# One order of the matmul queue for another in the memory loop: weights turned ahead of their products, activations turned between products, one gradient moved up, one product of zeros left out

## The reference

```python
def _mlp(params, h):
    for w1, w2 in params:
        h = h + jax.nn.gelu(h @ w1) @ w2
    return h
def assoc_loss(p, k, v):
    return jnp.mean((_mlp(p, k) - v) ** 2)
def step(carry, x_t):                       # 16 steps, one for each image row
    params, mom = carry                     # ((w1_0, w2_0), (w1_1, w2_1)), one set for each of 8 images
    k = _l2norm(x_t @ Wk); v = x_t @ Wv     # lr, forget, eta: means of sigmoids of x_t
    g = grad_fn(params, k, v)
    new_mom    = eta * mom - lr * g
    new_params = params * (1 - forget) + new_mom
(paramsT, _), _ = jax.lax.scan(step, (params0, mom0), x)
out = _mlp(mean of paramsT over the images, q)
```

## Time and profile before

| | |
|---|---|
| runs (3) | 324.80, 324.86, 325.09 us; median 324.86 |
| profiled execution | 322.84 us |
| its span, first to last instruction | 321.0 us (1.84 us lie around it) |
| memory loop in the span | 51.9 to 212.9 us, 16 steps |
| mean granted clock of PE | 0.979 of full speed |
| PE busy in the span | 280.7 us, 87% |

### The profile page before, as it was taken

The page is one execution under the profiler, slowest core; times in us unless marked ns, Lnnn a source line. Parts: engine busy times, 40 slices in busy tenths (PEclk is TensorE's granted clock), DMA queues, the critical chain, the costliest instruction groups (busy, mean ns, idle before and its releaser), DMA issues.

```text
span 321.0 us, 8491 instructions
## 1 busy us (share of the span) xinstructions
PE 280.7 (87%) x3338; PEld 186.9 (58%) x3345; DVE 212.1 (66%) x392; ACT 144.6 (45%) x353; POOL 145.6 (45%) x227
## 2 busy tenths in 40 slices
PE   8698759999999999999999999979985774899992
PEld 3233545777777777777777777754333552446642
DVE  0827554656666566665666656675478699899995
ACT  2003554466454664546655466523311662078511
POOL 8300087776667766677666776650000067200000
PEclk9999977999999999999999999999999998999998
DMA  7000000000000000000000000000000000000001
GB/s 289 14 0 2 0 1 2 0 0 0 0 0 0 0 0 0 0 0 0 0 0 0 0 0 0 0 2 2 0 0 2 0 2 0 1 2 0 0 0 65
DMA packets 874, 3.09 MB, mean 10 GB/s; under 512 B 96, under 2 KB 96, under 8 KB 864
## 3 DMA queue, kind: packets, MB, share of 16 engines
q1 hardware_dynamic: 864, 2.96, 2.5%
HBM read 2.44 MB, written 0.52 MB: 9 GB/s over the span
## 4 chain that ended last, share of the span: by engine, by line
PE 68%; DVE 23%; ACT 3%; issue 3%; POOL 2%; DVEq 0%; POOLq 0%
PE ps L1100 16%; PE ps L1082 9%; PE ps L1091 9%; PE ps L1110 6%; DVE arena_mem L754 4%; PE ps L1287 3%; PE ps L968 3%; PE ps L1318 2%; DVE arena_att L830 2%; PE ps L1166 2%; PE ps L993 2%; PE ps L1211 2%; DVE uf L850 1%; PE ps L1326 1%; ACT act_u L471 1%
## 5 line engine op out<-in xcount | busy, mean ns | idle before, releaser
L968 PE MATMUL ps<-zero 128*128 128x512 bf16 x130 | 34.7, 412 | 5.2 <-DVE uf L850 2.9
L350 POOL TENSOR_TENSOR arena_mem<-arena_mem,keep_e 128x512 f32<-128x512 f32 x32 | 33.4, 1043 | 0.0
L359 POOL TENSOR_TENSOR arena_mem<-arena_mem,keep_d 128x512 f32<-128x512 f32 x32 | 33.3, 1040 | 0.0
L747 DVE TENSOR_TENSOR arena_mem<-ps,arena_mem 128x512 f32<-128x512 f32 x49 | 32.0, 681 | 0.0
L481 ACT ACTIVATE arena_mem<-ps 128x512 f32<-128x512 f32 x48 | 28.7, 597 | 7.1 <-PE ps L1100 5.0
L1100 PE MATMUL ps<-const_sb,arena_mem 128*128 128x128 f32 x192 | 31.5, 287 | 0.0
L968 PEld LDWEIGHTS ps<-zero 128*128 128x128 bf16 x137 | 13.6, 106 | 24.6 <-issue 9.2
L471 ACT ACTIVATE act_u<-ps 128x128 f32<-128x128 f32 x32 | 8.9, 277 | 38.1 <-PE ps L1082 38.1
L366 POOL TENSOR_SCALAR z_e<-z_sq 128x128 f32<-128x128 f32 x32 | 9.5, 298 | 33.4 <-ACT z_sq L472 33.3
L1091 PE MATMUL ps<-act_u,arena_mem 128*64 128x16 f32 x512 | 20.6, 211 | 2.3
L1091 PEld LDWEIGHTS ps<-act_u,arena_mem 128*64 128x64 f32 x512 | 18.0, 137 | 7.7 <-issue 6.6
(11 more groups left out here) (267 smaller groups left out, 634.0 us busy)
## 6 DMA issues: line engine op xcount, KB each, us to landing
param_sb<-param SPq DMA_DIRECT2D x1, 840.5 KB, 7.2
arena_conv<-band SPq DMA_DIRECT2D x1, 576.0 KB, 5.6
xs_sb<-xs SPq DMA_DIRECT2D x1, 512.0 KB, 3.2
out<-xh SPq DMA_DIRECT2D x2, 256.0 KB, 2.1
const_sb<-const SPq DMA_DIRECT2D x1, 449.5 KB, 4.1
```

What stands on the lines that cost most here:

```text
L350: pool.tensor_tensor(qe[:, m, :].rearrange("p (b d) -> p b d", b=8), we[:, m, :].rearrange("p (b d) -> p b d", b=8), keep_e[:, bass.ts(t, ...
L359: pool.tensor_tensor(by_pair(kept), by_pair(w), keep_d[:, bass.ts(t, J)].unsqueeze(2).broadcast_to([P, J, E1]), ALU.mult).then_inc(sem("ke ...
L747: dve.tensor_tensor(by_pair(w11 if m == 1 else we[:, m, :]), momentum(m), by_pair(qe[:, m, :]), ALU.add)\
L968: pe.matmul(ps[:, bank, :], zero_bf[:, 0:P], zero_bf[:, :], start=True, stop=True)
```

## The change

On PE, in a step:

- w20 is turned right after z0, in the place of the product of zeros; w21 right after h1; w11 after h2. Each thus stands one product ahead of where a weight was turned, in another order of weights (w20, w21, w11 instead of w11, w21, w20), and the banks of PSUM are swapped.
- The activations are turned in pairs or singly: `u0`, `h1bd` after x; `u1`, `k_now` behind the turn of w11; `rbd` after `plus`. So `tok_lr` now holds u1 in the place of rbd, and `tok_raw` gets rbd by an ACT copy of its own (`r_tok`) and two others together.
- `plus` waits for `y1` instead of `slope1`, since the tanh of the second layer now goes to SBUF (`z_t1`) instead of PSUM.
- g21 stands ahead of the turn of `dhbd`; the other three gradients stay behind du0.

On DVE `updated(2)` goes ahead of the first `arg`, `updated(1)` moves from the end of a step into the next one, and the `mom_scale`s stand in another order. On POOL w21 is decayed before w11. ACT's copies follow PE's new order. The first w11 is now made by an update from its kept copy, like the first w21.

PE from z0 to x, first before and then of the change; `arena_mem` holds the weights, and the waits of each piece stand with its first row.

The diff, cut to its core:

```diff
@@ POOL, before the loop
-            pool.tensor_copy(by_pair(w11), ...).then_inc(sem("w11_new"), 1)
+            pool.tensor_copy(by_pair(qe[:, 1, :]), ...).then_inc(sem("kept_w11_new"), 1)
@@ POOL
                 kept_hidden(0, "w20_new")
+                kept_hidden(2, "w21_new")
                 kept_channels(qe[:, 1, :], w11, "w11_new", t + 1)
-                kept_hidden(2, "w21_new")
@@ ACT
                 hidden(0, "z0_done", "u0_ready", "z0_sq")
+                turned(7, 0, "w20_tp", "w20_d", -0.5)
                 evicted(h1bd[:, :], 5, 0, "h1_ps", "h1_ready")
-                turned(6, 1, "w11_tp", "w11_e")
+                turned(6, 2, "w21_tp", "w21_d", -0.5)
                 hidden(1, "z1_done", "u1_ready", "z1_sq")
-                turned(7, 2, "w21_tp", "w21_d", -0.5)
+                tanh(0, z_t0[:, 0, :], "y0", "tanh0")
                 evicted(rbd[:, :], 5, 0, "h2_ps", "r_ready")
                 tanh(1, th1, "y1", "tanh1")
-                tanh(0, z_t0[:, 0, :], "y0", "tanh0")
-                turned(6, 0, "w20_tp", "w20_d", -0.5)
+                turned(7, 1, "w11_tp", "w11_e")
                 act.wait_ge(sem("lr_tp"), t + 1)
-                act.activation(tok_lr[:, :, :], ps[:, 7, :]...
+                act.activation(tok_lr[:, :, :], ps[:, 6, :]...
+                evicted(tok_raw[:, 0, :], 7, 0, "r_tp", "r_tok")
                 evicted(dhbd[:, :], 4, 3 * P, "dh1_ps", "dh1_ready")
                 act.wait_ge(sem("raw_tp"), t + 1)
-                act.activation(tok_raw[:, 0:3, :], ps[:, 6, 0:3 * P]...
+                act.activation(tok_raw[:, 1:3, :], ps[:, 7, P:3 * P]...
-                evicted(dh_tok[:, :], 7, 0, "dh1_tp", "dh_tok")
+                evicted(dh_tok[:, :], 6, 0, "dh1_tp", "dh_tok")
@@ DVE
+                updated(2, "w21_new", "g21", t + 1)
                 arg(0, "z0_sq", "y0")
-                updated(2, "w21_new", "g21", t + 1)
+                updated(1, "w11_new", "g11", t + 1)
                 mom_scale(1)
+                mom_scale(2)
                 arg(1, "z1_sq", "y1")
-                mom_scale(2)
+                mom_scale(0)
...
                 mom_scale(3)
-                mom_scale(0)
...
                 updated_w10(t + 1)
                 updated(0, "w20_new", "g20", t + 1)
-                updated(1, "w11_new", "g11", t + 1)
             updated(2, "w21_new", "g21", NS + 1)
+            updated(1, "w11_new", "g11", NS + 1)
@@ PE
                 pe.wait_ge(sem("kbd_ready"), 4)
-                fill(7, 0, BANK)
                 pe.wait_ge(sem("w20_new"), t + 1)
+                turn_weights(7, we[:, 0, :]).then_inc(sem("w20_tp"), 1)
                 pe.wait_ge(sem("u0_ready"), t + 1)
                 by_image(5, 0, we[:, 0, :], act_u[:, 0, :]).then_inc(sem("h1_ps"), 1)
+                pe.wait_ge(sem("w21_new"), t + 1)
+                turn_weights(6, we[:, 2, :]).then_inc(sem("w21_tp"), 1)
+                pe.wait_ge(sem("x_now"), t + 1)
+                pe.wait_ge(sem("y0"), t + 1)
                 pe.wait_ge(sem("w11_new"), t + 1)
-                turn_weights(6, w11).then_inc(sem("w11_tp"), 1)
-                pe.wait_ge(sem("y0"), t + 1)
                 pe.wait_ge(sem("h1_ready"), t + 1)
                 by_halves(4, P, w11, h1bd).then_inc(sem("z1_done"), 1)
-                pe.wait_ge(sem("x_now"), t + 1)
-                pe.wait_ge(sem("w21_new"), t + 1)
-                turn_weights(7, we[:, 2, :]).then_inc(sem("w21_tp"), 1)
...
+                pe.wait_ge(sem("w21_d"), t + 1)
+                for n, x in enumerate((act_u[:, 0, :], h1bd)):
+                    turn(6, n * P, x[:, :])
                 pe.wait_ge(sem("u1_ready"), t + 1)
                 by_image(5, 0, we[:, 2, :], act_u[:, 1, :]).then_inc(sem("h2_ps"), 1)
-                pe.wait_ge(sem("w11_e"), t + 1)
-                turn_weights(6, we[:, 0, :]).then_inc(sem("w20_tp"), 1)
-                pe.wait_ge(sem("w21_d"), t + 1)
+                pe.wait_ge(sem("w20_d"), t + 1)
+                turn_weights(7, w11).then_inc(sem("w11_tp"), 1)
+                turn(6, 2 * P, act_u[:, 1, :])
+                turn(6, 3 * P, k_now[:, :]).then_inc(sem("lr_tp"), 1)
                 pe.wait_ge(sem("r_ready"), t + 1)
                 by_halves(5, 2 * P, wd[:, 2, :], rbd).then_inc(sem("du1_done"), 1)
-                for n, x in enumerate((act_u[:, 0, :], h1bd, rbd, k_now)):
-                    mm = turn(7, n * P, x[:, :])
-                mm.then_inc(sem("lr_tp"), 1)
-                pe.wait_ge(sem("slope1"), t + 1)
+                pe.wait_ge(sem("y1"), t + 1)
                 plus(4, 3 * P, rbd[:, :], True)
+                pe.wait_ge(sem("w11_e"), t + 1)
+                turn(7, 0, rbd[:, :]).then_inc(sem("r_tp"), 1)
                 pe.wait_ge(sem("dz1_ready"), t + 1)
                 by_image(4, 3 * P, we[:, 1, :], dz1).then_inc(sem("dh1_ps"), 1)
-                pe.wait_ge(sem("w20_d"), t + 1)
-                turn(6, 0, act_u[:, 1, :])
-                turn(6, P, dz1[:, :])
+                pe.wait_ge(sem("r_tok"), t + 1)
+                turn(7, P, dz1[:, :])
                 pe.wait_ge(sem("slope0"), t + 1)
-                turn(6, 2 * P, z_p[:, 0, :]).then_inc(sem("raw_tp"), 1)
+                turn(7, 2 * P, z_p[:, 0, :]).then_inc(sem("raw_tp"), 1)
                 pe.wait_ge(sem("tok_lr"), t + 1)
+                pe.wait_ge(sem("scaled"), 4 * t + 4)
+                gradient(2, u1_lr, tok_raw[:, 0, :]).then_inc(sem("g21"), 1)
                 pe.wait_ge(sem("dh1_ready"), t + 1)
-                turn(7, 0, dhbd[:, :]).then_inc(sem("dh1_tp"), 1)
+                turn(6, 0, dhbd[:, :]).then_inc(sem("dh1_tp"), 1)
...
                 pe.wait_ge(sem("tok_raw"), t + 1)
-                pe.wait_ge(sem("scaled"), 4 * t + 4)
                 gradient(1, h1_lr, tok_raw[:, 1, :]).then_inc(sem("g11"), 1)
-                gradient(2, tok_raw[:, 0, :], r_lr).then_inc(sem("g21"), 1)
```

More of the change, by code:

```diff
@@ L193, in conv_attn_scan_kernel @@
         z_t0 = sb("z_t0", [P, 2, P])
+        z_t1 = sb("z_t1", [P, P])
         h1bd = sb("h1bd", [P, P])
@@ L226, in by_pair @@
             return buf.rearrange("p (j n) -> p j n", n=P)
-        th1 = ps[:, 4, P:2 * P]
+        th1 = z_t1[:, :]
         def columns_first(buf):
@@ L316, in _ @@
                                  par("mats_e")[:, n * C:(n + 1) * C].unsqueeze(1).broadcast_to([P, 8, C])).then_inc(sem(done), 1)
-            pool.tensor_copy(by_pair(w11), par("w1_1").unsqueeze(1).broadcast_to([P, J, E1])).then_inc(sem("w11_new"), 1)
+            pool.tensor_copy(by_pair(qe[:, 1, :]), par("w1_1").unsqueeze(1).broadcast_to([P, J, E1])).then_inc(sem("kept_w11_new"), 1)
             def inverse_norm(out, squares, clipped, n):
@@ L488, in _ @@
                 hidden(0, "z0_done", "u0_ready", "z0_sq")
+                turned(7, 0, "w20_tp", "w20_d", -0.5)
                 evicted(h1bd[:, :], 5, 0, "h1_ps", "h1_ready")
-                turned(6, 1, "w11_tp", "w11_e")
+                turned(6, 2, "w21_tp", "w21_d", -0.5)
                 hidden(1, "z1_done", "u1_ready", "z1_sq")
-                turned(7, 2, "w21_tp", "w21_d", -0.5)
+                tanh(0, z_t0[:, 0, :], "y0", "tanh0")
                 evicted(rbd[:, :], 5, 0, "h2_ps", "r_ready")
                 tanh(1, th1, "y1", "tanh1")
-                tanh(0, z_t0[:, 0, :], "y0", "tanh0")
-                turned(6, 0, "w20_tp", "w20_d", -0.5)
+                turned(7, 1, "w11_tp", "w11_e")
                 act.wait_ge(sem("lr_tp"), t + 1)
-                act.activation(tok_lr[:, :, :], ps[:, 7, :].rearrange("p (s n) -> p s n", s=4), ACT.Copy,
+                act.activation(tok_lr[:, :, :], ps[:, 6, :].rearrange("p (s n) -> p s n", s=4), ACT.Copy,
                                scale=lrn[:, bass.ds(t, 1)]).then_inc(sem("tok_lr"), 1)
+                evicted(tok_raw[:, 0, :], 7, 0, "r_tp", "r_tok")
                 evicted(dhbd[:, :], 4, 3 * P, "dh1_ps", "dh1_ready")
                 act.wait_ge(sem("raw_tp"), t + 1)
-                act.activation(tok_raw[:, 0:3, :], ps[:, 6, 0:3 * P].rearrange("p (s n) -> p s n", s=3), ACT.Copy)\
+                act.activation(tok_raw[:, 1:3, :], ps[:, 7, P:3 * P].rearrange("p (s n) -> p s n", s=2), ACT.Copy)\
                    .then_inc(sem("tok_raw"), 1)
-                evicted(dh_tok[:, :], 7, 0, "dh1_tp", "dh_tok")
+                evicted(dh_tok[:, :], 6, 0, "dh1_tp", "dh_tok")
                 act.activation(k_now[:, :], k_all[:, bass.ds(t * P + P, P)], ACT.Copy).then_inc(sem("k_now"), 1)
@@ L1070, in _ @@
                 mm = pe.matmul(ps[:, bank, :], zero_bf[:, 0:P], zero_bf[:, :], start=True, stop=True)
+                if bank == 0:
+                    mm.then_inc(sem("g11"), 1)
             mm.then_inc(sem("g21"), 1)
@@ L1168, in _ @@
                 mm.then_inc(sem("du0_done"), 1)
-                u0_lr, h1_lr, r_lr, k_lr = (tok_lr[:, i, :] for i in range(4))
                 pe.wait_ge(sem("tok_raw"), t + 1)
-                pe.wait_ge(sem("scaled"), 4 * t + 4)
```

(1 more changed line is left out.)

1 line of the change is left out of this document (added).

## The result

| | before | changed |
|---|---|---|
| runs | 323.87, 324.80, 324.86, 325.09 us | 332.41, 334.78, 338.84, 356.75 us |
| median | 324.83 us | 336.81 us |
| profiled execution, span | 322.84, 321.0 us | 332.41, 330.6 us |
| mean granted clock | 0.979 | 0.942 |
| memory loop from z0 | 51.88 to 212.9: 161.0 us | 51.59 to 220.8: 169.2 us |

The change made the kernel slower: 1.0275 of the time before [1.0214, 1.0337]. Forecast were 324.0 us and a range of 322.7 to 325.5. Ratios here leave out the executions that lie more than 1.5% above the fastest of the same kernel, which in this case are those that lost most clock, so a ratio near 1 says nothing of the falls, and all times are listed beside it.

A forecast was written before the change was run, and what follows sets the result against it. The loop, 161 us of the span, was taken as a PE queue with few holes. 15 steps gaining 0.06 each give 0.9, so 322.84 becomes 321.9; plus 2.0 to the median makes 324.0 us, range 322.7 to 325.5.

The forecast's parts named there:

- The account of a step: PE's pieces in one loop step: next z0 at 9.99 us instead of 10.05, a gain of 0.06 a step.
- h1 at 1.24: Start of piece h1 behind z0 in a step: 1.24 us, 0.11 later than before, with w20's turn already done.
- dh1 at 6.12: Start of piece dh1 behind z0: 6.12 us, as it waits for dz1, a hole of 0.05 us.
- The first step I count as nothing: First loop step: no gain, since POOL's work for q makes the slope late and dz1 as late as before.
- The 2.0 us that the sum adds: Whole kernel: the median of the runs lies 2.0 us above the profiled execution, added to 321.9.
- Rival 5: Loop on PE: one product of zeros fewer, clock falls from 2.4 to 1.2 GHz for one step, 333 us; chance 0.05.
- at most 9 us: Upper size of the clock-fall loss: one step of 16 with PE's 9.2 us up to doubled, giving 333 us.
- paid for by g21 at 0.44 in the place of 0.22: g21 alone ahead of dhbd's turn moves the next piece by 0.44 us, against 0.22 in the row of four.
- a wait of 0.06 to 0.2: Before the change, PE's hole ahead of dhbd's turn, waiting for ACT: 0.06 to 0.2 us, expected gone.

The follow-up runs named there:

- e1: Changed kernel with its one product of zeros ahead of z0 issued twice; 323.36 to 358.72 us, ratio 1.0002 to the kernel before.
- e2: Kernel before without its second product of zeros, the one behind z0; 323.87 to 331.66 us, ratio 1.0022.
- f2b: Changed kernel with PE made to wait idle ahead of the loop for POOL's spread of q, repeat run; 332.88 to 346.83 us, no ratio.
- j2: Changed kernel with PE's idle wait ahead of the loop and the removed product of zeros put back behind z0; 334.29 to 350.04 us, ratio 1.0384.
- e4: Changed kernel with the removed product of zeros put back behind z0; 323.27 to 339.29 us, ratio 0.9997 to the kernel before.
- j1: Kernel before without its second product of zeros, with PE's idle wait ahead of the loop; 332.41 to 335.04 us, ratio 1.0282.
- j3: Changed kernel with PE's idle wait ahead of the loop and the turns of u0, h1bd, u1, k_now together behind du1; 335.43 to 360.28 us, no ratio.
- e3: Changed kernel with 14 more products of zeros right ahead of the loop; 322.60 to 325.43 us, ratio 0.9992 to the kernel before.
- g1: Changed kernel with POOL's spread of q moved behind the loop; 321.13 to 322.72 us, ratio 0.9897 to the kernel before.
- j4: Changed kernel with PE's idle wait ahead of the loop and g21 back behind g11; 329.52 to 331.06 us, ratio 1.0171.
- k1: Changed kernel with g21 back behind g11 and no other edit; 320.38 to 326.70 us, ratio 0.9888 to the kernel before.
- k2: Changed kernel with g21 back behind g11 and POOL's spread of q behind the loop; 318.05 to 322.29 us, ratio 0.9833 to the kernel before.
- h1: Kernel before with POOL's spread of q moved behind the loop; 322.10 to 324.09 us, median 323.15, ratio 0.9939.

## Why the prediction was wrong

- **The account of a step was right.** 9.98 against 9.99, each piece within 0.04. The holes that it named are the ones there: h1 at 1.24, dh1 at 6.12.
- **The step that failed: "The first step I count as nothing ... dz1 then comes as late as before."** dh1 started 7.69 behind z0 instead of 6.52, since PE's start against POOL's work for q is not fixed: the spread began 1.0 us behind z0 in the profile of before, 2.2 in that of after, 3.4 in e1, 2.2 in e2, as the clock ahead of the loop was low for 6.8, 3.4, 0 and 3.4 us. One profiled execution, which happened to start the loop late, was read as if all started alike. The 2.0 us that the sum adds from that execution to the median may well be this hole in the others, though no profile of before shows it. And of the four turns that covered this wait between du1 and `plus` one is left there, so that PE runs dry at 6.12 and not at 6.5. dh1 waited 1.57 us, the clock fell behind it for 20.5 us, and the first step cost 2.66 us and the second 6.45.
- **Rival 5 was what happened, at a chance of 0.05.** What was argued against it, 16.5 us of turns at granted clock 1.00, shows that this stretch of turns kept 1.00; it says nothing of what a hole sets off in the loop. The size failed as well: "at most 9 us", to 333, fits the profiled execution, not the other three of 334.78, 338.84 and 356.75. A low step costs 16.5 - 9.98 = 6.5 us, and several follow each other: 20.5 us low were seen in the changed kernel, 54.6 in f2b and 58.0 in j2.
- **Not what the rival named.** Neither the product of zeros (e1, e4, j1, j2) nor the place of the four turns that j3 moves decides. "TensorE: Matmul & The Clock Gate", Part 4, in the Trainium skill says that turns don't count as busy PE in the same way; the trace does not bear it out, with 16.5 us of 90 turns and nothing else at 1.00. The loops of e3 and g1 have every turn of the change and keep 1.00 in their profiles.
- **The move of g21 was weighed wrongly as a part.** The text has it "paid for by g21 at 0.44 in the place of 0.22" against a wait of 0.06 to 0.2, and never gives the sum of that edit alone. Measured it costs 9.98 - 9.81 = 0.17 a step, 2.7 us in 16, which hid most of what the other edits gain (10.05 - 9.81 = 0.24 a step). It is also what the long low stretches come with.
- **Open.** Why a lone gradient keeps PE low longer, and why the stretches differ so among executions of one kernel, no run tells. What the runs show is that with this edit undone none of the 17 executions of j4, k1 and k2 took more than 331.1 us. Nor do they tell why the hole of 0.63 us in h1 and the gap of 1.36 us behind the loop in the profile of before passed without a fall.

## What to carry to other kernels

Look at the first turn of a loop by itself: other engines may still be busy with work from outside it, and an order that spreads out the cover of a wait is exposed there first. Check how far the start moves between executions before counting on a margin of a microsecond, and price a hole by what the clock then costs, not by its own length. Cost each moved piece alone, and run the change with each edit undone: here one edit of several hid a gain of 1.1%.

## What the runs showed of the hardware

- PE was busy without a break and stayed at 1.2 GHz, for 20.5 us in the changed kernel, for 51.0 of the 54.6 us of the low stretch in f2b and for 54.3 of 58.0 in j2 (the rest was the idle time at its start).
- The length of a hole did not tell the length of the low stretch: 2.81 us and 6.8 (e1), 1.57 and 20.5 (the changed kernel), 1.14 and 3.4 (e2), 1.04 and 3.4 (k2), 0.63 and none (h1).
- The clock ahead of the loop went with what its first step met: with 6.8 us, 3.4 us and nothing of low clock there, POOL's spread began 1.00, 2.19 and 3.41 us behind z0 (before, after, e1).
- A step wholly at 1.2 GHz took 16.1 to 16.9 us instead of 9.8 to 10.2 (j4 16.06 against 9.81, j2 16.90 against 10.08), 1.6 to 1.7 times as long.
